# Two layers of scan, routed experts and retention on one core: own places in the first routed layer, and another order in the retention loop

## The chip, the cores and the metric

The kernel runs on one core of a Trainium2 chip. The metric is the device time of one execution in microseconds. Engines are named as in the profile: PE (TensorE), PEld (its weight loads), DVE (VectorE), ACT (ScalarE), POOL (GpSimd), SP (SyncE, which here only issues DMAs).

## The reference

An input of 8 sequences of 256 tokens with 128 features (2048 tokens) goes through two layers. Each layer normalizes its input to `xn` and adds two branches.

```
layer 0:  x = x + ssm(xn) + moe0(xn)
  ssm : up-projection, causal conv, silu, scan over 256 steps with 256 x 16 states, gate, down-projection
  moe0: scores = softmax(xn @ Wr)            # 8 experts
        G, idx = top_k(scores.T, 512)        # each EXPERT chooses 512 tokens
        h   = gelu(xn[idx] @ W1 + b1)        # 128 -> 512, per expert
        out[idx] += G * (h @ W2 + b2)        # 512 -> 128
layer 1:  x = x + retention(xn) + moe1(xn)
  retention: 8 heads of 16, q k v projections, scores = (q k^T) * decay mask, scores @ v,
             normalization per head, silu gate, output projection
  moe1: 16 experts, each token takes its best 2, relu, 128 -> 512 -> 128
```

## The kernel before

All five engines have programs written out by hand, each in the order of its code, and they meet at semaphores only. No scheduler decides anything. The stages follow each other: norms and the expert search of layer 0, the scan (one batch after another, 16 steps each, DVE the busiest), the first routed layer (moe0), layer 1's norm, retention, and the second routed layer.

**The first routed layer.** For expert e the steps are these. `one_hot(e)` on DVE (L505) compares the 16 x 8 places of the tokens with a row of numbers and writes a bf16 tile `hot[e]` of 128 x 2048. `compact(e)` on PE (L1010) multiplies it in 16 small matmuls into bank 7, which gives 512 token numbers. `indices(e)` on DVE (L513) adds and casts them into `idx`. `gather(e, q)` on POOL (L1633), four indirect DMAs of 128 rows each, brings the rows of `token_rows` (features and the 8 gates) into `xg`. `turn_rows(e)` on PE (L1088) transposes them into bank 6, and `rows_out(e)` on ACT copies them to `xgT`. `up0(e)` on PE (L1097) writes banks 0 to 3, `gelus(e)` on ACT makes `hbuf` of them, and `down0(e)` on PE (L1108) writes bank 4 or 5. `gated(e)` on DVE (L556) adds the bias row and multiplies by the gate into `ye` (two buffers). `put(e)` on POOL (L1686), four indirect DMAs, scatters `ye` into expert e's own table `expert_rows` in DRAM, which was zeroed earlier. `rows_in(e)` on SP (L831) loads that table of 1 MB back into one of two buffers, and `row_sum(e)` on DVE (L565) adds it to `acc`.

What sets the order is `expert_steps`, which runs a list of (lag, function) for s = 2 to 10 and calls each function with s - lag; every engine has its own list:

```
PE    turn_rows(0), then ((2, up0), (0, compact), (1, turn_rows), (3, down0))
DVE   ((0, one_hot), (0, indices), (3, gated), (5, row_sum))
ACT   rows_out(0), then ((2, gelus), (1, rows_out))
POOL  ((0, gathers), (3, put))
```

Experts 0 and 1 are compacted and gathered while the last batch of the scan still runs. Places are shared: `hot` has four (two in `xnT`, two in `gate`), so that `one_hot(e)` for e > 3 waits for `compact(e - 2)`; `xg` has four in `xm`, so that `gather(e)` for e > 3 waits for `gated(e - 4)`; weights and bias rows have two. SP loads the weights of expert e when expert e - 2 has let go of them (`weights1`, `weights2`, L792 and L797), in between the `rows_in`. The result of the scan is turned back by PE (L1086) in four groups through banks 0 and 1, and DVE adds it to `acc` (L552).

**Retention.** Per batch b: `project(b)` on PE (L1143) makes q and k in bank 4; ACT's `qk_out(b)` (L1481) copies them out; DVE's `query_decay(b)` (L682) takes its part; `scores(b)` on PE (L1155) writes banks 0 to 3; DVE's `decay(b, j)` (L690, four of them) multiplies by the mask into `pm`; `retain(b)` on PE (L1177) multiplies by v; ACT's `ret_out(b)` (L1500) copies it out. `scores(b)` waits until the four `decay(b - 1, j)` are done. In the loop PE runs scores(b), retain(b - 1), project(b + 1).

## Time and profile before

| | us |
|---|---|
| median of three runs | 796.07 (795.64 to 796.97) |
| the profiled execution | 797.28 |
| its span in the trace | 795.4 |
| scan's last down-projection leaves ACT | at 427.0 |
| first routed layer, to its last scatter | 427.0 to 538.6 |
| norm and projections of layer 1 | to 565 |
| routing of layer 1 on DVE | to 589 |
| retention | 589 to 660 |
| second routed layer and output | 660 to 795.4 |

The profiled execution lies 1.2 us above the median; 1.9 us of it lie outside the span. "Busy" is the time of instructions on an engine. For POOL it is the time in which it makes a DMA's descriptors, not the transfer. A row of the timeline gives start, duration, engine, line, operation and tiles, then the idle time before it and what ended that.

### The profile page before, as it was taken

How to read it: one execution, taken by the hardware profiler on the slowest of the kernel's cores; microseconds unless marked ns; L12 is line 12 of the kernel's file. 1: busy time of each engine (PE TensorE's matmuls, PEld its weight loads, DVE VectorE, ACT ScalarE, POOL GpSimd, SP SyncE). 2: the span in 40 equal slices, each digit the busy share in tenths (PEclk: the TensorE clock that was granted, in tenths of full speed). 3: DMA queues.
4: the chain of work that ended last, by engine and by line, in shares of the span. 5: the costliest groups of instructions: out<-in, count | busy, mean ns of one | idle time of the engine just before them, and what ended most of it. 6: DMA issues, size and time to landing. Idle time of an engine off the chain costs nothing.

```text
span 795.4 us, 12651 instructions
## 1 busy us (share of the span) xinstructions
PE 578.7 (73%) x3363; PEld 420.2 (53%) x3364; DVE 560.2 (70%) x1342; ACT 295.6 (37%) x706; POOL 392.6 (49%) x481
## 2 busy tenths in 40 slices
PE   4368874698888899879687776751637747999991
PEld 3222333466565666556464554641525426999991
DVE  7256589899999999999995225157475375665553
ACT  2532363664453546445312313120414432334430
POOL 1030036477676767767744578572137500444441
PEclk9999995899999999999796889785859975999996
DMA  9996000000000000000003346549501110212115
GB/s 187 210 315 189 1 3 0 2 0 2 1 1 0 0 0 0 0 0 0 1 5 115 91 132 198 158 135 316 205 15 51 45 27 5 57 48 55 50 30 158
DMA packets 59174, 55.83 MB, mean 70 GB/s; under 512 B 7871, under 2 KB 46166, under 8 KB 58880
## 3 DMA queue, kind: packets, MB, share of 16 engines
q1 hardware_dynamic: 53744, 43.61, 19.0%
q0 software_dynamic: 5392, 11.76, 5.8%
q8 instruction: 17, 0.28, 0.1%
q14 instruction: 21, 0.17, 0.1%
HBM read 35.27 MB, written 21.12 MB: 71 GB/s over the span
## 4 chain that ended last, share of the span: by engine, by line
PE 36%; DVE 31%; issue 6%; POOL 3%; DMA 3%; ACT 2%; DVEq 1%; SPq 1%; ACTq 0%; POOLq 0%
DVE arena L529 13%; PE bank L1287 7%; PE bank L1273 6%; DVE arena L490 6%; PE bank L1115 3%; PE bank L1038 3%; PE bank L1008 2%; PE bank L1040 2%; POOL expert_rows L1693 2%; DVE hbuf L725 2%; DMA xm<-token_rows,zbuf 2%; PE bank L978 1%; PE bank L1105 1%; POOL xm L1640 1%; PE bank L1166 1%
## 5 line engine op out<-in xcount | busy, mean ns | idle before, releaser
L529 DVE TENSOR_TENSOR_SCAN arena<-bank,arena 128x256 f32<-128x256 f32 x256 | 162.3, 679 | 5.2 <-issue 5.2
L1648 POOL TENSOR_TENSOR arena<-arena 128x256 f32<-128x256 f32 x128 | 99.4, 777 | 93.2 <-DVE arena L490 89.8
L1413 ACT ACTIVATE arena<-delta,nega 128x256 f32<-128x256 f32 (+1 forms) x256 | 107.7, 496 | 30.4 <-DVE arena L529 28.6
L490 DVE SCALAR_TENSOR_TENSOR arena<-arena,inva,bank 128x256 f32<-128x256 f32 x256 | 109.2, 471 | 0.0
L1038 PE MATMUL bank<-bd,xnw 128*128 128x258 f32 x256 | 88.6, 429 | 26.4 <-DVE arena L529 26.0
L1735 POOL DMA_INDIRECT pair_rows<-w1b,xnT x48 | 49.8, 1037 | 98.5 <-DVE w1b L761 95.2
L1008 PE MATMUL bank<-arena,ident 128*128 128x256 f32 x256 | 80.3, 398 | 20.3 <-DVEq L503 15.7
L1040 PE MATMUL bank<-bd,xnw 128*128 128x256 f32 x256 | 79.4, 393 | 0.0
L1629 POOL TENSOR_TENSOR bd<-cfs,btok 128x258 f32<-128x258 f32 x128 | 77.8, 628 | 0.0
L1038 PEld LDWEIGHTS bank<-bd,xnw 128*128 128x128 f32 x256 | 44.2, 198 | 56.0 <-DVE arena L529 40.4
L1008 PEld LDWEIGHTS bank<-arena,ident 128*128 128x128 f32 x256 | 44.6, 198 | 29.0 <-POOL arena L1648 25.2
L1287 PE MATMUL bank<-arena,hbuf 128*128 x384 | 56.5, 291 | 0.0
L1040 PEld LDWEIGHTS bank<-bd,xnw 128*128 128x128 f32 x256 | 50.9, 199 | 8.2
L1273 PE MATMUL bank<-xsT,xm 128*128 128x128 f32 x384 | 53.0, 283 | 0.9 <-DVE xm L744 0.9
L1693 POOL DMA_INDIRECT expert_rows<-gate,zbuf x32 | 41.0, 1281 | 22.9 <-DVE gate L563 14.3
L1273 PEld LDWEIGHTS bank<-xsT,xm 128*128 128x128 f32 x384 | 48.3, 198 | 1.9 <-DVE xm L744 1.8
L1287 PEld LDWEIGHTS bank<-arena,hbuf 128*128 128x128 f32 x384 | 47.3, 194 | 3.3
L1640 POOL DMA_INDIRECT xm<-token_rows,zbuf x32 | 39.0, 1219 | 18.3 <-DVE zbuf L517 9.7
L743 DVE COPY xm<-bd 128x512 f32 x48 | 20.6, 429 | 33.4 <-issue 31.0
L561 DVE TENSOR_TENSOR gate<-bank,zbuf 128x512 f32<-128x512 f32 x8 | 5.5, 692 | 51.6 <-PE bank L1115 51.4
L1115 PEld LDWEIGHTS bank<-w2b,hbuf 128*128 128x128 f32 x256 | 36.7, 232 | 0.5 <-issue 0.5
L1115 PE MATMUL bank<-w2b,hbuf 128*128 128x128 f32 x256 | 36.7, 314 | 0.0
(273 smaller groups left out, 1033.9 us busy)
## 6 DMA issues: line engine op xcount, KB each, us to landing
expert_rows<-bd SPq DMA_DIRECT2D x8, 1024.0 KB, 9.8
bd<-in_w SPq DMA_DIRECT2D x4, 1024.0 KB, 14.4
arena<-in_w SPq DMA_DIRECT2D x4, 1024.0 KB, 14.2
slots_in<-bd POOLq DMA_DIRECT2D x1, 3120.0 KB, 34.4
xnT<-slots_in SPq DMA_DIRECT2D x48, 65.0 KB, 1.8
w1b<-in_w SPq DMA_DIRECT2D x8, 256.0 KB, 6.4
w2b<-in_w SPq DMA_DIRECT2D x8, 256.0 KB
delta<-in_mask_d SPq DMA_DIRECT2D x1, 1664.0 KB
```

The costliest lines, as they stand in the source:

```text
L490: m = V.scalar_tensor_tensor(out=zb[:, s % 8, r, :], in0=zb[:, s % 8, r, :], scalar=inva[:, h, n:n + 1], in1=c_bank(n2)[:, r * L:(r + 1) * ...
L529: m = V.tensor_tensor_scan(zb[:, s % 8, r, :], dw_bank(par, s)[:, r * L:(r + 1) * L], abar[:, s % 8, r, :], 0.0, ALU.add, ALU.mult)
L1008: pe.matmul(Y[:, h * L:(h + 1) * L], ident[:, :], zb[:, s % 8, 0, :], start=(s == 0), stop=(s == 15), skip_group_check=True).then_inc(S["p ...
L1038: pe.matmul(o[:, :, 0:P + 1], xT[:, par, 0, h * P:(h + 1) * P], bd[:, par, 0, 2 * n2:2 * n2 + 2, :], start=True, stop=False, skip_group_ch ...
L1040: pe.matmul(o[:, :, P:L], xT[:, par, 1, h * P:(h + 1) * P], bd[:, par, 1, 2 * n2:2 * n2 + 2, 0:P], start=False, stop=True, skip_group_chec ...
L1115: m = pe.matmul(bank[4 + e % 2][:, q * P:(q + 1) * P], hbuf[:, e % 2, c, q * P:(q + 1) * P], w2b[:, e % 2, c, :], start=(c == 0), stop=(c ...
L1273: m = pe.matmul(bank[2 * (u % 2) + c // 2][:, c % 2 * P:(c % 2 + 1) * P], w1s[:, u % 2, c * P:(c + 1) * P], xsT[:, u % 2, :], start=True, ...
L1287: m = pe.matmul(bank[6 + u % 2][:, 0:P], hT[:, u % 2, c * P:(c + 1) * P], w2r[:, bass.ds(e, 1), c, :], start=False, stop=(c == HC - 1))
L1413: m = nc.scalar.activation(abar[:, s % 8, r, :], delta[:, h, bass.ds(b * L, L)], ACT.Exp, scale=negs[:, h, n:n + 1])
L1629: m = nc.gpsimd.tensor_tensor(bd[:, par, c, n, :], bid[:, None, :].broadcast_to([P, 2, P + 1]), btok[:, par, c, n, None].broadcast_to([P, ...
L1648: nc.gpsimd.tensor_tensor(zb[:, s % 8, 0, :], zb[:, s % 8, 0, :], zb[:, s % 8, 1, :], ALU.add).then_inc(S["q_ready"], 1)
L1693: nc.gpsimd.indirect_dma_start(out=moe[e], out_offset=bass.IndirectOffsetOnAxis(ap=idx[:, 4 * e + q:4 * e + q + 1], axis=0), in_=ye[:, e % ...
```

## The change

1. Routed layer: `hot[2]` to `hot[7]` get own places in `arena`, `xg[2]` to `xg[7]` own places in `bd`, and the weights of experts 2 to 5 own places in the other half of `bd`; SP loads those four when batch 6 of the scan has left `bd` (`dw_ready` at 7 x 16). Experts 6 and 7 take the places of 0 and 1. All eight bias rows come in one load, `b2r`. The waits that the shared places needed are gone.
2. DVE: `one_hot(2)` stands ahead of the four additions to `acc`; the other one-hots and indices follow at once, and only behind the last of them `gated` and `row_sum`.
3. PE: the turned result of the scan goes through four banks (2 to 5), so that its groups don't wait for DVE; the six compactions stand between the first steps of experts 0 and 1, and from expert 2 on the order is up0(e), turn_rows(e + 1), down0(e - 1).
4. POOL: gathers of experts 2, 3 and 4, then put(0), gathers of 5, put(1), gathers of 6, put(2), gathers of 7, put(3), and put(4) to put(7).
5. SP: `rows_in(0)` to `rows_in(7)` in a row, behind the loads of experts 6 and 7.
6. Retention: PE runs scores(b), project(b + 1), retain(b - 1); ACT runs qk_out(b), ret_out(b - 2), values_out(b).

The diff's core:

```diff
-        b2b = zf[:, 640:640 + 2 * P].rearrange("p (a d) -> p a d", a=2)
+        b2r = arena[:, 6144:6144 + E0 * P].rearrange("p (e d) -> p e d", e=E0)
...
-        xg = [xmf[:, o:o + 4 * ROW].rearrange("p (q r) -> p q r", q=4) for o in (0, 4 * ROW, T, 8 * ROW)]
+        bdf = bd[:, :, :, :, :].rearrange("p a c n t -> p (a c n t)")
+        xg = [f.rearrange("p (q r) -> p q r", q=4) for f in
+              [xmf[:, o:o + 4 * ROW] for o in (0, 4 * ROW)] + [bdf[:, 4128 + 4 * ROW * k:4128 + 4 * ROW * (k + 1)] for k in range(E0 - 2)]]
-        hots = [f.bitcast(BF16).rearrange("p (a t r) -> p a t r", a=2, t=NT) for f in (xnT[:, :], gate[:, 0, :])]
-        hot = [hots[e > 1][:, e % 2, :, :] for e in range(E0)]
+        hot = [f[:, o:o + NT * P // 2].bitcast(BF16).rearrange("p (t r) -> p t r", t=NT) for f, o in
+               [(xnT, 0), (xnT, NT * P // 2)] + [(arena, NT * P // 2 * k) for k in range(E0 - 2)]]
+        w1e = [w1b[:, e % 2, :] if e % 6 < 2 else bdf[:, 1024 * e - 2048:1024 * e - 1536] for e in range(E0)]
+        w2e = [w2b[:, e % 2, :, :] if e % 6 < 2 else
+               bdf[:, 1024 * e - 1536:1024 * e - 1024].rearrange("p (c d) -> p c d", c=HC) for e in range(E0)]
...
-                if e > 3:
-                    dve.wait_ge(S["cp_ready"], e - 1)
...
+            one_hot(2)
...
-                V.tensor_tensor(t, t, bank[q % 2][:, :], ALU.add).then_inc(S["dve_done"], 1)
+                V.tensor_tensor(t, t, bank[YM_BANK[q]][:, :], ALU.add).then_inc(S["dve_done"], 1)
...
+                if e == 0:
+                    dve.wait_ge(S["b2_in"], 16)
...
-                                     b2b[:, e % 2, None, :].broadcast_to([P, 4, P]), ALU.add))
-                V.tensor_tensor(y, y, xg[e % 4][:, :, P + e:P + e + 1].broadcast_to([P, 4, P]), ALU.mult).then_inc(S["ye_ready"], 1)
+                                     b2r[:, e, None, :].broadcast_to([P, 4, P]), ALU.add))
+                V.tensor_tensor(y, y, xg[e][:, :, P + e:P + e + 1].broadcast_to([P, 4, P]), ALU.mult).then_inc(S["ye_ready"], 1)
...
-            expert_steps(((0, one_hot), (0, indices), (3, gated), (5, row_sum)))
+            for e in range(AHEAD, E0):
+                indices(e)
+                if e + 1 < E0:
+                    one_hot(e + 1)
+            expert_steps(((3, gated), (5, row_sum)))
...
-            def weights1(e):
...
-            def weights2(e):
-                if e > 1:
-                    sp.wait_ge(S["ye_ready"], e - 1)
...
+            def weights(e):
+                mid = 1 < e < 6
+                if e > 5:
+                    sp.wait_ge(S["u_ready"], (e - 5) * HC)
+                sp.dma_start(w1e[e], w1_0[e, :, :]).then_inc(S["w_mid" if mid else f"w1_in{e % 2}"], 16)
+                if e > 5:
+                    sp.wait_ge(S["ye_ready"], e - 5)
+                sp.dma_start(w2e[e].rearrange("p c d -> p (c d)"), w2_0[e, :, :]).then_inc(S["w_mid" if mid else f"w2_in{e % 2}"], 16)
...
+            sp.wait_ge(S["dw_ready"], 7 * 16)
+            for e in range(2, 6):
+                weights(e)
...
             sp.wait_ge(S["dve_done"], 7)
+            sp.dma_start(b2r, b2_0.rearrange("e d -> (e d)").partition_broadcast(P).rearrange("p (e d) -> p e d", e=E0)
+                         ).then_inc(S["b2_in"], 16)
...
-
-            weights1(2)
-            for e in range(2, E0):
-                if e + 1 < E0:
-                    weights1(e + 1)
-                weights2(e)
-                rows_in(e - 2)
-            rows_in(E0 - 2)
-            rows_in(E0 - 1)
+                        sp.dma_start(staged[e % 2][:, 4 * q:4 * q + 4, :], src[:, 4 * q:4 * q + 4, :]).then_inc(S[f"pair_in{q}"], 16)
+
+            weights(6)
+            weights(7)
+            for e in range(E0):
+                rows_in(e)
...
-                pe.wait_ge(S["dve_done"], 3 if q < 2 else 2 + q)
+                if q == 0:
+                    pe.wait_ge(S["dve_done"], 3)
...
-                    else:
-                        pe.wait_ge(S["dve_done"], 7)
-                    pe.matmul(bank[c][:, :], w1b[:, e % 2, c * P:(c + 1) * P], xgT[:, e % 2, :], start=True, stop=True
+                    elif c > 1:
+                        pe.wait_ge(S["dve_done"], 4 + c)
...
-            expert_steps(((2, up0), (0, compact), (1, turn_rows), (3, down0)))
+            compact(2)
+            up0(0)
+            compact(3)
+            turn_rows(1)
+            compact(4)
+            up0(1)
+            compact(5)
+            pe.wait_ge(S["dve_done"], 7)
+            down0(0)
+            compact(6)
+            turn_rows(2)
+            compact(7)
+            for e in range(2, E0):
+                up0(e)
+                if e + 1 < E0:
+                    turn_rows(e + 1)
+                down0(e - 1)
+            down0(E0 - 1)
...
                     scores(b, par)
+                    project(i * 2 + (3 + par))
                     retain(i * 2 + (1 + par), 1 - par)
-                    project(i * 2 + (3 + par))
...
                     b = i * 2 + (2 + par)
+                    qk_out(b, par)
                     ret_out(i * 2 + par, par)
-                    qk_out(b, par)
...
-                    if e > 3:
-                        pool.wait_ge(S["ye_ready"], e - 3)
...
-            expert_steps(((0, gathers), (3, put)))
+            for e in range(AHEAD, E0):
+                for q in range(4):
+                    gather(e, q)
+                if e > 3:
+                    put(e - 4)
+            for e in range(E0 - 4, E0):
+                put(e)
```

Three places where the order of instructions moves.

POOL in the first routed layer, from the gathers of expert 3 on (`xm` and `bd` hold `xg`; `gate` holds `ye`). Before:

```order
L1640 DMA xm<-token_rows,zbuf 128x136 [waits id_ready,rows_g]
L1640 DMA xm<-token_rows,zbuf 128x136 x3
L1693 DMA expert_rows<-gate,zbuf 2048x128 [waits ye_ready]
L1693 DMA expert_rows<-gate,zbuf 2048x128 x3
L1640 DMA xm<-token_rows,zbuf 128x136 [waits ye_ready,id_ready,rows_g]
L1640 DMA xm<-token_rows,zbuf 128x136 x3
```

With the change:

```order
L1669 DMA bd<-token_rows,zbuf 128x136 [waits id_ready,rows_g]
L1669 DMA bd<-token_rows,zbuf 128x136 x3
L1718 DMA expert_rows<-gate,zbuf 2048x128 [waits ye_ready]
L1718 DMA expert_rows<-gate,zbuf 2048x128 x3
L1669 DMA bd<-token_rows,zbuf 128x136 [waits id_ready,rows_g]
L1669 DMA bd<-token_rows,zbuf 128x136 x3
```

The gathers of expert 4 stand ahead of the first scatter and wait for indices only; from expert 5 on gathers and scatters alternate as before, but one expert further on.

PE in the first routed layer, from `turn_rows(0)` on (L1094 and L1104 are `turn_rows`, L1019 and L1028 `compact`, L1105 and L1118 `up0`, L1115 and L1129 `down0`). Before:

```order
L1094 MATMUL bank<-ident,xm 128x128 [waits xg_in0]
L1094 MATMUL bank<-ident,xm 128x128 x3
L1105 MATMUL bank<-xm,w1b 128x512 [waits dve_done,xg_sb,w1_in0]
L1105 MATMUL bank<-xm,w1b 128x512 [waits dve_done] x3
L1019 MATMUL bank<-zbuf,gate 128x8 [waits id_ready,hot_ready]
L1019 MATMUL bank<-zbuf,gate 128x8 x15
L1094 MATMUL bank<-ident,xm 128x128 [waits xg_sb,xg_in1]
L1094 MATMUL bank<-ident,xm 128x128 x3
```

With the change:

```order
L1104 MATMUL bank<-ident,xm 128x128 [waits xg_in0]
L1104 MATMUL bank<-ident,xm 128x128 x3
L1028 MATMUL bank<-zbuf,arena 128x8 [waits id_ready,hot_ready]
L1028 MATMUL bank<-zbuf,arena 128x8 x15
L1118 MATMUL bank<-xm,w1b 128x512 [waits xg_sb,w1_in0]
L1118 MATMUL bank<-xm,w1b 128x512
L1118 MATMUL bank<-xm,w1b 128x512 [waits dve_done] x2
L1028 MATMUL bank<-zbuf,arena 128x8 [waits id_ready,hot_ready]
```

The first compaction now stands ahead of `up0(0)`, and down0(0) has four compactions ahead of it.

PE in the retention loop (L1166 and L1197 are `scores`, L1191, L1195, L1222 and L1226 `retain`, L1152 and L1183 `project`). Before:

```order
L1159 ISA [waits qk_sb]
L1166 MATMUL bank<-xm,w1b 128x128 [waits pm_ready]
L1166 MATMUL bank<-xm,w1b 128x128 x15
L1182 ISA
L1191 MATMUL bank<-zbuf,xm 32x128 [waits vs_sb,r_free,qd_sb,pm_ready]
L1191 MATMUL bank<-zbuf,xm 32x128 x15
L1195 MATMUL bank<-xm 32x128 x4
L1152 ISA [waits qd_sb]
L1152 MATMUL bank<-xnT,z2p 128x256 x2
```

With the change:

```order
L1190 ISA [waits qk_sb]
L1197 MATMUL bank<-xm,w1b 128x128 [waits pm_ready]
L1197 MATMUL bank<-xm,w1b 128x128 x15
L1183 ISA [waits qd_sb]
L1183 MATMUL bank<-xnT,z2p 128x256 x2
L1213 ISA
L1222 MATMUL bank<-zbuf,xm 32x128 [waits vs_sb,r_free,qd_sb,pm_ready]
L1222 MATMUL bank<-zbuf,xm 32x128 x15
L1226 MATMUL bank<-xm 32x128 x4
```

`project` has moved in between `scores` and `retain`.

## Rows read from the trace of the kernel before

**Rows 1.** The page: busy time of the engines over the span.

```profile
PE 578.7 (73%) x3363; PEld 420.2 (53%) x3364; DVE 560.2 (70%) x1342; ACT 295.6 (37%) x706; POOL 392.6 (49%) x481
```

**Rows 2.** Busy time by stretch: us, five engines, granted clock, DMA share, GB/s.

```profile
437.00:540.00 103.00, 67.77 (x416) 52.10 (x416) 37.40 (x38) 24.12 (x35) 71.75 (x56) 0.85 0.48 147
...
597.00:625.00 28.00, 19.43 (x412) 15.14 (x416) 14.34 (x27) 13.28 (x36) 20.20 (x24) 0.99 0.15 49
```

**Rows 3.** Waits, 431 to 540 us: engine, line, for whom; total, times, longest.

```profile
DVE gate L561 <- PE bank L1115: 51.4, 7, 12.0
...
POOL expert_rows L1693 <- DVE gate L563: 14.3, 4, 7.7
```

**Rows 4.** Groups of instructions, 431 to 540 us: busy, mean ns, idle before.

```profile
L1693 POOL DMA_INDIRECT expert_rows<-gate,zbuf x32 | 41.0, 1281 | 22.9 <-DVE gate L563 14.3 <-issue 8.5
...
L1640 POOL DMA_INDIRECT xm<-token_rows,zbuf x24 | 30.8, 1284 | 16.4 <-DVE zbuf L517 9.7 <-issue 6.1 <-DVE gate L563 0.6
...
L510 DVE TENSOR_TENSOR gate<-cfs,zbuf 128x2048 bf16<-128x2048 f32 x6 | 13.7, 2286 | 0.3 <-DVE acc L568 0.2
...
L568 DVE TENSOR_TENSOR acc<-acc,xnT 128x2048 f32<-128x2048 f32 x4 | 9.1, 2287 | 4.0 <-DMA xnT<-expert_rows 4.0
```

**Rows 5.** Timeline, from the end of the scan to the gathers of expert 2.

```profile
427.04 3.53 PE L1086 MATMUL bank<-ident,z2p 128*128 128x128 f32 x16 [0.65 <-ACT z2p L1403]
...
430.41 0.60 PE L1094 MATMUL bank<-ident,xm 128*128 128x128 f32 x4
...
435.25 0.55 PE L1019 MATMUL bank<-zbuf,gate 128*128 128x8 bf16 x16
...
436.95 2.27 POOL L1640 DMA_INDIRECT xm<-token_rows,zbuf  x1 [9.41 <-DVE zbuf L517]
```

**Rows 6.** Timeline, 440 to 470 us, PE, DVE and POOL.

```profile
445.05 1.12 PE L1094 MATMUL bank<-ident,xm 128*128 128x128 f32 x4 [3.97 <-DMA xm<-token_rows,zbuf]
...
445.95 5.94 PE L1115 MATMUL bank<-w2b,hbuf 128*128 128x128 f32 x32
...
456.50 3.74 PE L1115 MATMUL bank<-w2b,hbuf 128*128 128x128 f32 x32
...
460.07 3.60 PE L1105 MATMUL bank<-xm,w1b 128*128 128x512 f32 x8
...
461.61 2.28 DVE L510 TENSOR_TENSOR gate<-cfs,zbuf 128x2048 bf16<-128x2048 f32 x1
...
461.86 2.87 POOL L1640 DMA_INDIRECT xm<-token_rows,zbuf  x1 [0.30 <-DVE gate L563]
```

**Rows 7.** Timeline, the last scatter, and the sum behind it.

```profile
537.67 0.97 POOL L1693 DMA_INDIRECT expert_rows<-gate,zbuf  x1 [0.30 <-issue]
...
542.77 0.69 DVE L579 TENSOR_TENSOR acc<-acc,xnw 128x512 f32<-128x512 f32 x1 [1.19 <-DMA xnw<-expert_rows]
```

**Rows 8.** Timeline, one turn of the retention loop.

```profile
604.61 1.17 PE L1166 MATMUL bank<-xm,w1b 32*128 32x128 f32 x32 [1.45 <-ACT xm L1488]
...
605.72 1.08 PE L1191 MATMUL bank<-hbuf,xm 128*32 128x128 f32 x32
605.80 2.48 DVE L695 TENSOR_TENSOR zbuf<-bank,delta 128x512 f32<-128x512 f32 x4 [0.99 <-PE bank L1166]
606.48 0.96 POOL L1727 DMA_INDIRECT slots_in<-xnw,slot  x1 [0.30 <-issue]
...
606.95 1.13 PE L1152 MATMUL bank<-xnT,z2p 128*128 x4
...
608.57 0.83 ACT L1488 ACTIVATE xm<-bank,parity 128x256 f32<-128x256 f32 x2
...
609.53 1.17 PE L1166 MATMUL bank<-xm,w1b 32*128 32x128 f32 x32 [1.46 <-ACT xm L1488]
```

**Rows 9.** Timeline, `scores(1)`, ahead of the loop.

```profile
592.60 2.09 PE L1166 MATMUL bank<-xm,w1b 32*128 32x128 f32 x32 [1.54 <-DVE hbuf L695]
```

45 lines of the change are left out of this document (20 added, 25 removed).

## The prediction

> **What bounds the kernel now.** The page's busy shares come first [rows 1]: no engine is busy over three quarters of the span, so the stages must be read one by one. The view by stretch [rows 2] shows that in the first routed layer (437 to 540 us) POOL is the fullest engine, 71.75 us of 103, and PE has 67.77 at a granted clock of 0.85. POOL's work there is 24 gathers and 32 scatters [rows 4]. Next I read what it waits for [rows 3]: 14.3 us until DVE's `gated` has made rows to scatter, in 4 waits, the longest 7.7. DVE itself waits 51.4 us for `down0`. So neither engine is full: POOL stands still while an expert passes through PE, and PE stands still while POOL gathers the next one, since gather(e) stands behind put(e - 3) in POOL's order. After the stage everything hangs on the last scatter: it is issued at 537.67, and the last table's first quarter is in the sum at 542.77 [rows 7].
>
> The same rows give the price of a POOL DMA. One lasts 0.96 us and the next begins 0.30 later [rows 6, 8], so 1.27 us each. The mean is 1.28 us of busy time [rows 4], so something lengthens some of them. Rows 6 show what: DVE's L510 runs from 461.61 to 463.89, and the gather that begins at 461.86 takes 2.87 us, to 464.73, that is 0.84 us past the end of L510. L510 and L568 read two SBUF tiles for 2.29 us [rows 4]; when a POOL DMA begins within one, it starts its work at that one's end. DVE's L695 reads a PSUM bank, and the scatter at 606.48, inside its 2.48 us, takes its plain 0.96 [rows 8]. Of 71.8 us of POOL's busy time, 56 x 0.965 = 54.0 are its own and 17.8 are such holds, for 5 one-hots and 6 row sums that meet it, 1.6 us each.
>
> The Trainium skill bears on this (SBUF — State Buffer, section Who interferes with whom). It says that a DVE instruction with two SBUF inputs contends only with a GpSimd instruction that reads SBUF, and infers that a `tensor_tensor` leaves descriptor generation alone, since that needs the write port. By that inference the 17.8 us of holds would not exist, and the stream below would end at 506 instead of 524. The trace of before disagrees (2.87 us against 0.96), so the sum keeps them.
>
> **The routed layer, step by step.** From POOL's view the stage before is 436.95 to 538.64, 101.7 us: 71.1 for 56 DMAs at 1.27, 17.8 of holds, and 12.8 of waits.
>
> *Start.* Before, `compact(2)` begins on PE at 435.25 and POOL's first gather of expert 2 at 436.95, 1.70 later [rows 5]. Ahead of it stood `up0(0)`, and the one-hot behind DVE's four additions. Now `one_hot(2)` runs before the additions, and `compact(2)` stands right behind `turn_rows(0)`. The 16 transposes run from 427.04, and `turn_rows(0)` from 430.41 for 0.60 [rows 5]; four banks in place of two can only shorten that, I count nothing. 431.0 + 1.7 = 432.7: 4.25 us earlier. `one_hot(2)` now holds one of the gathers of expert 1, which lie before that and have slack.
>
> *Gathers first.* The gathers of 2, 3 and 4 need only indices. DVE makes those in a chain with PE: one-hot 2.29, compact 0.55, add and cast 0.4. Expert 3's indices come behind `up0(0)` (about 436.2), expert 4's some 3.4 us after (439.8), ahead of POOL in both cases. POOL takes 12 x 1.27 = 15.2 us plus four or five holds of 1.6, to about 455. Will put(0) be ready? `up0(1)` now waits for `compact(4)` to 439.1, `down0(0)` follows at about 443.2 and takes 3.74 or 5.94 us by the clock [rows 6]; `compact(6)`, `one_hot(7)` and `compact(7)` then stand ahead of `gated(0)` on DVE, which ends at 452.6 to 454.8. So its wait is about zero. This order makes `gated(0)` later than before (453.35), at no cost, since POOL has gathers to do.
>
> *The rest of the stream.* From then on POOL has 16 + 28 more DMAs. An expert costs PE 3.60 + 0.60 + 3.74 = 7.9 us at the high clock [rows 5, 6], POOL 10.2 us for a gather and a put and more with holds. So POOL is last. `gated(e)` needs put(e - 2) landed; that is one put and one gather away, and holds POOL up at most for moments. Of 12.8 us of waits I leave 2.5; the ends are 0 and 8. The holds stay at 17.8: as many one-hots (3 to 7) and row sums (0 to 5) meet the stream. If every one of the 11 hit fully it would be 25; if half missed, 9.
>
> Sum: 432.7 + 71.1 + 17.8 + 2.5 = 524.1 against 538.64, **14.5 us less**. Behind the last scatter nothing changes: `rows_in(7)`, quarters, norm. It would give back a little if the loads of 1 MB fell behind the faster puts; put after put takes 5.1 to 7 us, and the load of a table some 5.
>
> *Edits at nothing.* The 2 MB of weights for experts 2 to 5 load during batch 7 of the scan, where SP has nothing else; if they were late, `up0(2)` would wait, 90 us after their issue. The bias load goes ahead of the mask's 1.7 MB and delays it 2 us, needed 100 us later; `gated(0)`, the first to wait for the bias, comes 20 us after its issue. Experts 6 and 7 load in turns when 0 and 1 are through, 20 us and more before use. SP's `rows_in(0)` stands behind these two waits; `row_sum(0)` stands behind `gated(2)` anyway. Fewer semaphores and banks 2 to 5: `up0(0)` and `down0(0)` wait for the additions, which end before.
>
> **Retention.** One turn is 609.53 - 604.61 = 4.92 us [rows 8]: scores, from 605.72 `retain`, from 606.95 `project`, ACT's copies to 609.40, then the next scores. `retain` is in that chain for 1.23 us and feeds nothing in it. With `project` in front the chain is 1.11 + 2.58 = 3.69. Now the next in line: scores(b + 1) wait for the four `decay(b)`, which run from 605.80 to 608.28 [rows 8]; with 0.15 of signal that is 3.82 to 3.92 from scores to scores. PE's own work is 1.11 + 1.23 + 1.13 = 3.5 plus gaps of 0.2, also below. So a turn takes about 3.9, 1.0 less, in the 5 turns from scores(2) to scores(7): **5.0 us less**; the ends are 3 and 6. The 32 scatters of POOL there end at 632, well ahead of their use. What follows (gates, norm per head, projection) begins at the last `retain` and moves along whole.
>
> **The sum**: 14.5 + 5.0 = 19.5 us. Against the profiled execution 797.28 - 19.5 = 777.8; its own time is 1.2 us above the median, and against the median 796.07 the forecast is 776.6.
>
> **The rivals.**
> 1. *PE bounds the routed layer at its low clock.* Compactions and waits for rows leave gaps; before, the granted clock was 0.85 [rows 2], and after a wait of 3.97 us a `down0` took 5.94 and a turn 1.12 [rows 6]. From 439.1: 7 x 3.60 + 8 x 5.94 + 6 x 1.12 + 4 for compactions = 83.5, to 522.6, then `gated` and a last put of 8: 531. Gain 7.6 + 5.0: 783.5. Against it: such gaps mean that PE has time to spare. 0.16.
> 2. *The gathers meet the mask's load.* Twelve gathers in a row start with its transfer, before only after most of it. If POOL had to wait until it is through (about 441), 8 us are lost: 784.6. Before, gathers during it kept their pace. 0.05.
> 3. *Retention gains nothing*, since DVE or ACT in order takes `retain`'s place: 781.6. 0.07.
> 4. *More than I count*: no waits left, half of the holds missed: 524.1 - 2.5 - 5 = 516.6, and 6 from retention: 768. 0.05.
> 5. *Slower: PE at 1.2 GHz in the retention loop.* scores(1) took 2.09 us ahead of the loop [rows 9] against 1.17 within, where the granted clock was 0.99 [rows 2]. If the new order let it fall, PE's 3.5 us of a turn become 6.2 and with gaps 6.6, 1.7 x 6 = 10 us more; with rival 1's gain of 7.6 that is 798.5. It decides when the loop's granted clock is below about 0.6. Against it: PE is busier than before in every turn. 0.02. The Trainium skill (TensorE: Matmul & The Clock Gate, Part 1) has it that activity releases the throttle, so by it the loop would keep the high clock.
> 6. *It changes nothing*, because rows come back in step with the loads of 1 MB: 0.01.
>
> **How the numbers follow.** The forecast has 0.64. Its own bounds (waits 0 to 8, holds 9 to 25, retention 3 to 6) rarely add up and give 771 to 784. With rivals 1 to 3 on the high side and 4 on the low one, the range for 8 in 10 is 770.5 to 785. 0.2% (1.6 us) is about what a measurement of this kernel tells from no change: faster 0.97, same 0.01, slower 0.02.
>
> **What would show it.** The first gather of expert 2 at about 432.7 of the span; 12 gathers in a row; no POOL wait for `gated` over 3 us; POOL's long DMAs still ending 0.84 us after a two-input DVE instruction; the last scatter's end at 524; scores to scores 3.9 us, with DVE's `decay` ending right before. Wrong it is if `down0` mostly takes 5.9 us and POOL waits for it (rival 1), if gathers of expert 2 are long with DVE idle (2), or if a turn stays at 4.9 (3).

## The result, and the profile after

| | before | changed |
|---|---|---|
| median of four runs, us | 796.08 (795.64 to 796.97) | 775.16 (773.63 to 776.99) |
| the profiled execution | 797.28 | 776.99 |
| its span | 795.4 | 775.2 |

The ratio of the runs is 0.9755, with a 95% interval of 0.9729 to 0.9782: 19.5 us less (17.4 to 21.6). The two medians by themselves are 20.9 apart, which this interval takes in. The forecast was 776.6, the range 770.5 to 785.

The profile after, in the order of the rows before. First the page's busy line and the view by stretch over the routed stage, cut where the first scatter starts (us; PE, PEld, DVE, ACT, POOL busy; granted clock, DMA share, GB/s):

```profile
PE 579.2 (75%) x3363; PEld 419.8 (54%) x3364; DVE 559.7 (72%) x1342; ACT 295.0 (38%) x706; POOL 393.5 (51%) x481
```
```profile
427.00:456.00 29.00, 23.63 (x182) 15.72 (x181) 17.52 (x24) 10.73 (x16) 21.42 (x14) 0.87 0.47 149
456.00:523.00 67.00, 46.95 (x286) 36.11 (x284) 23.49 (x20) 18.75 (x28) 52.78 (x45) 0.90 0.51 153
```

The busy times are those of [rows 1] within 1 us: no work was taken away. From 456 to 523 us POOL is busy 52.78 of 67 us, and its 45 DMAs leave a gap of 0.30 us each: it hardly stands still. PE is busy 46.95 of the 67. The waits and the groups from 427 to 522 us say so too (for each wait: engine and tile waiting, for whom; total, times, longest):

```profile
DVE gate L568 <- PE bank L1129: 21.5, 4, 7.5
...
POOL expert_rows L1718 <- issue: 9.5, 31, 0.3
```
```profile
L1718 POOL DMA_INDIRECT expert_rows<-gate,zbuf x32 | 40.7, 1270 | 10.5 <-issue 9.5 <-DVE gate L570 1.1
L1669 POOL DMA_INDIRECT bd<-token_rows,zbuf x24 | 31.2, 1299 | 10.9 <-issue 6.4 <-DVE zbuf L521 4.5
```

The scatters' wait for `gated` was 14.3 us in 4 waits [rows 3]; it is 1.1 in one. DVE's own wait for `down0` fell from 51.4 us to 21.5. What has not changed is the length of the DMAs: 1270 and 1299 ns are those of before [rows 4]. 40.7 + 31.2 - 56 x 0.965 = 17.9 us of holds (17.8 before).

The timeline at the start and the end of the stage:

```profile
427.69 0.47 ACT L1434 ACTIVATE z2p<-bank,colv 128x256 f32<-128x256 f32 x1 [21.90 <-PE bank L1086]
...
431.44 0.60 PE L1104 MATMUL bank<-ident,xm 128*128 128x128 f32 x4
...
431.88 0.55 PE L1028 MATMUL bank<-zbuf,arena 128*128 128x8 bf16 x16
...
433.58 2.26 POOL L1669 DMA_INDIRECT bd<-token_rows,zbuf  x1 [3.92 <-DVE zbuf L521]
```
```profile
448.38 2.29 DVE L514 TENSOR_TENSOR arena<-cfs,zbuf 128x2048 bf16<-128x2048 f32 x1
...
451.60 0.69 DVE L568 TENSOR_TENSOR gate<-bank,arena 128x512 f32<-128x512 f32 x1
```
```profile
449.00 2.50 POOL L1669 DMA_INDIRECT bd<-token_rows,zbuf  x1 [0.30 <-issue]
...
456.85 1.00 POOL L1718 DMA_INDIRECT expert_rows<-gate,zbuf  x1 [0.30 <-issue]
...
509.82 0.97 POOL L1718 DMA_INDIRECT expert_rows<-gate,zbuf  x1 [1.07 <-DVE gate L570]
...
521.99 0.97 POOL L1718 DMA_INDIRECT expert_rows<-gate,zbuf  x1 [0.31 <-issue]
```

`compact(2)` stands right behind `turn_rows(0)`, and the first gather of expert 2 begins 433.58 - 431.88 = 1.70 us after it, as before. The gather at 449.00 begins within the one-hot of 448.38 to 450.67 and ends at 451.50, 0.83 after it: the hold of [rows 6]. `gated(0)` starts at 451.60, 5.25 us before POOL comes to its scatter at 456.85; the only wait in the whole stream is the 1.07 before 509.82.

The retention loop, PE and then DVE:

```profile
599.27 1.17 PE L1197 MATMUL bank<-xm,w1b 32*128 32x128 f32 x32 [0.36 <-DVE zbuf L706]
600.37 1.13 PE L1183 MATMUL bank<-xnT,z2p 128*128 128x256 f32 x4
601.43 1.08 PE L1222 MATMUL bank<-zbuf,xm 128*32 128x128 f32 x32
602.33 0.40 PE L1226 MATMUL bank<-xm 128*32 128x128 f32 x8
603.06 1.17 PE L1197 MATMUL bank<-xm,w1b 32*128 32x128 f32 x32 [0.33 <-DVE hbuf L706]
```
```profile
600.43 2.49 DVE L706 TENSOR_TENSOR hbuf<-bank,delta 128x512 f32<-128x512 f32 x4 [1.09 <-PE bank L1197]
602.87 0.29 DVE L699 TENSOR_TENSOR xm<-bank,delta 128x128 f32<-128x128 f32 x1
```

A turn is 603.06 - 599.27 = 3.79 us against 4.92 [rows 8]. The scores waited for ACT's L1488 before; now they wait for DVE: `decay` ends at 602.92, 0.14 before them.

Where the time went, with `scan` for the start of ACT's last down-projection copy (427.69 above). The first five rows are spans from one event to the next and the sixth what follows; together they are the difference of the spans, 795.4 - 775.2.

| stretch | before | after | |
|---|---|---|---|
| start to scan | 426.51 | 427.69 | +1.2 |
| scan to first gather of expert 2 | 10.44 | 5.89 | -4.5 |
| that gather to the last scatter's end | 101.7 | 89.4 | -12.3 |
| last scatter's end to the first projection of retention | 50.4 | 50.7 | +0.3 |
| that projection to the gates, behind the loop | 40.7 | 35.0 | -5.7 |
| gates to the end | 165.7 | 166.6 | +0.9 |

In the fourth stretch 0.9 us are given back at once: from the last scatter's end to L590's first addition 5.04 us pass, against 4.13 for L579 [rows 7].

### The profile page after: what moved, and what is told of

Same layout as the page of the kernel before. It is cut to its first block, busy times and chain, and to the rows that moved or that the text cites. A ratio compares the mean times of both kernels' runs of the same rounds, so it can differ in the third digit from the quotient of the medians.

```text
span 775.2 us, 12645 instructions
## 1 busy us (share of the span) xinstructions
PE 579.2 (75%) x3363; PEld 419.8 (54%) x3364; DVE 559.7 (72%) x1342; ACT 295.0 (38%) x706; POOL 393.5 (51%) x481
## 4 chain that ended last, share of the span: by engine, by line
PE 33%; DVE 29%; POOL 8%; issue 7%; DMA 3%; ACT 2%; DVEq 1%; SPq 1%; POOLq 0%; ACTq 0%
DVE arena L533 12%; PE bank L1318 7%; PE bank L1304 6%; DVE arena L496 5%; POOL expert_rows L1718 4%; PE bank L1047 4%; PE bank L1017 3%; POOL bd L1669 3%; PE bank L1049 3%; DVE hbuf L736 2%; PE bank L987 1%; DMA xnw<-expert_rows 1%; PE bank L1197 1%; DVE hbuf L706 1%; PE bank L1316 1%
## 5 line engine op out<-in xcount | busy, mean ns | idle before, releaser
L1017 PE MATMUL bank<-arena,ident 128*128 128x256 f32 x256 | 81.9, 405 | 20.3 <-DVEq L509 15.7
L1049 PE MATMUL bank<-bd,xnw 128*128 128x256 f32 x256 | 81.5, 402 | 0.0
L1047 PEld LDWEIGHTS bank<-bd,xnw 128*128 128x128 f32 x256 | 45.8, 202 | 51.1 <-DVE arena L533 35.3
L1017 PEld LDWEIGHTS bank<-arena,ident 128*128 128x128 f32 x256 | 45.4, 201 | 29.2 <-POOL arena L1677 25.2
L1049 PEld LDWEIGHTS bank<-bd,xnw 128*128 128x128 f32 x256 | 52.4, 205 | 8.7
L1718 POOL DMA_INDIRECT expert_rows<-gate,zbuf x32 | 40.7, 1270 | 10.5 <-issue 9.5
L1669 POOL DMA_INDIRECT bd<-token_rows,zbuf x24 | 31.2, 1299 | 10.9 <-issue 6.4
L907 PE MATMUL bank<-ident,xnw 128*128 128x128 f32 x32 | 7.9, 394 | 38.2 <-DVEq L327 38.2
L1758 POOL DMA_INDIRECT slots_in<-xnw,slot x32 | 30.7, 961 | 9.9 <-issue 9.2
L955 PE MATMUL bank<-z2p,delta 128*128 x64 | 34.9, 672 | 0.0
```

The source lines that it names most:

```text
L1017: pe.matmul(Y[:, h * L:(h + 1) * L], ident[:, :], zb[:, s % 8, 0, :], start=(s == 0), stop=(s == 15), skip_group_check=True).then_inc(S["p ...
L1047: pe.matmul(o[:, :, 0:P + 1], xT[:, par, 0, h * P:(h + 1) * P], bd[:, par, 0, 2 * n2:2 * n2 + 2, :], start=True, stop=False, skip_group_ch ...
L1049: pe.matmul(o[:, :, P:L], xT[:, par, 1, h * P:(h + 1) * P], bd[:, par, 1, 2 * n2:2 * n2 + 2, 0:P], start=False, stop=True, skip_group_chec ...
L1669: nc.gpsimd.indirect_dma_start(out=xg[e][:, q, :], out_offset=None, in_=rows, in_offset=bass.IndirectOffsetOnAxis(ap=idx[:, 4 * e + q:4 * ...
L1718: nc.gpsimd.indirect_dma_start(out=moe[e], out_offset=bass.IndirectOffsetOnAxis(ap=idx[:, 4 * e + q:4 * e + q + 1], axis=0), in_=ye[:, e % ...
```

## The experiments

Twelve kernels ran, in three groups. `ret_alone` is an edit of the kernel before, `control` the changed kernel itself, the others edits of the changed kernel; each stood beside runs of the kernel before on its chip. That kernel's median was 793.71 us beside `ret_undone`, `ret_pe_only`, `pool_undone` and `compact_undone`, 796.75 beside `ret_alone`, `weights_late`, `no_row_sum` and `quarters` (another chip), and 793.18 beside the last four. So medians compare within such a group only, and across groups the ratios do. The stage numbers of their profiled executions, taken as above ("last" is the end of the last scatter after the scan's end; "holds" is POOL's busy time for the 56 DMAs less 56 x 0.965; "turn" is the mean from scores to scores in the loop):

| kernel | scan | first gather | last | holds | turn | median | ratio to before (95%) |
|---|---|---|---|---|---|---|---|
| before | 426.5 | 10.4 | 112.1 | 17.8 | 4.9 | 796.08 | |
| changed | 427.7 | 5.9 | 95.3 | 17.9 | 3.8 | 775.16 | 0.9755 (0.9729 to 0.9782) |
| ret_undone | 424.9 | 6.6 | 96.0 | 18.5 | 4.9 | 778.51 | 0.9796 (0.9758 to 0.9834) |
| ret_pe_only | 423.8 | 6.0 | 96.9 | 19.4 | 5.2 | 780.39 | 0.9824 (0.9790 to 0.9859) |
| ret_alone | 427.4 | 10.4 | 111.8 | 18.0 | 3.8 | 791.00 | 0.9934 (0.9908 to 0.9960) |
| pool_undone | 422.8 | 5.9 | 101.9 | 18.4 | 3.8 | 779.42 | 0.9830 (0.9786 to 0.9873) |
| compact_undone | 423.8 | 10.3 | 106.5 | 12.7 | 3.8 | 783.66 | 0.9870 (0.9833 to 0.9907) |
| weights_late | 423.9 | 5.9 | 96.4 | 18.9 | 3.8 | 775.07 | 0.9755 (0.9704 to 0.9806) |
| no_row_sum | 428.5 | 5.9 | 86.6 | 8.4 | 3.8 | 767.46 | 0.9649 (0.9599 to 0.9700) |
| control | 424.5 | 5.9 | 96.1 | 18.7 | 3.8 | 775.52 | 0.9770 (0.9749 to 0.9792) |
| quarters | 426.0 | 6.6 | 90.6 | 4.5 | 3.8 | 772.34 | 0.9711 (0.9649 to 0.9773) |
| rows_quarters | 423.4 | 6.6 | 90.2 | 9.9 | 3.8 | 770.62 | 0.9722 (0.9706 to 0.9738) |
| hots_quarters | 426.0 | 6.6 | 93.8 | 10.6 | 3.8 | 772.05 | 0.9731 (0.9707 to 0.9756) |
| gated_early | 423.8 | 6.6 | 87.1 | 4.0 | 3.8 | 767.24 | 0.9669 (0.9656 to 0.9682) |

The first thing to see is the scan's column. None of these edits touches the scan's instructions, and its end lies anywhere from 422.8 to 428.5; the changed kernel itself has 427.7 in one execution and 424.5 in another (`control`). So a difference of 3 us between two medians may be the scan's, and the columns behind it, which count from its end, tell more. The same holds for ratios: the changed kernel has 0.9755 in its own runs and 0.9770 as `control`. What an edit costs is given below against 0.9755; against `control` each such figure is 0.15%, or 1.2 us, smaller.

The first gather is at 5.9 in some of these kernels and at 6.6 in others, also where the edit lies elsewhere (`ret_undone`). It goes with PE's clock: in the 29 us from the scan's end the mean granted clock was 0.87 in the changed kernel and in `control`, and 0.79 in `ret_undone` and `quarters`. There `turn_rows(0)` took 1.06 us in place of 0.60.

### Retention: both orders back, one order back, and the orders alone

`ret_undone`, the loop's part on each engine (the peeled end alike):

```diff
                     scores(b, par)
-                    project(i * 2 + (3 + par))
                     retain(i * 2 + (1 + par), 1 - par)
+                    project(i * 2 + (3 + par))
...
-                    qk_out(b, par)
                     ret_out(i * 2 + par, par)
+                    qk_out(b, par)
```

> The changed kernel with both orders of the retention loop put back (PE: scores, retain, project; ACT: ret_out, qk_out, values_out), the routed layer left as changed. Theory: the turn from scores to scores goes from 3.80 us back to about 4.9, and the time rises by 5.4 us over the changed kernel, to about 780.6; the routed layer's last scatter stays where it is. Rival (the retention loop was only a bystander, and its shorter turns come from something ahead of it): the turn stays at 3.8 and the time at 775.

`ret_pe_only` has the second hunk alone:

> The changed kernel with ACT's order in the retention loop put back (ret_out ahead of qk_out), and PE's new order kept. Theory: qk_out of batch b then waits behind ret_out of the batch before, which PE's new order makes late, so the next scores wait for both; the turn goes to 5.3 us or so, slower than with both orders old (4.9), and the time to about 782.7. Rival (the order on ACT is irrelevant, PE's order makes the gain): the turn stays at 3.8 and the time at 775.

`ret_alone` is the kernel before with both hunks the other way round:

> The kernel before with the retention loop's two new orders alone; the routed layer is as it was. Theory: the turn falls from 4.88 us to 3.8 and the time by 5.4 us, to about 790.7, so that this part of the change and the routed part add up to the whole. Rival (the two parts meet, the gain needs the other part): 796 or 793.

Measured: turns of 4.88 us in `ret_undone` (4.83 to 4.92), 5.18 in `ret_pe_only` (5.13 to 5.22), 3.80 in `ret_alone`. PE and ACT in `ret_pe_only`:

```profile
597.22 0.38 ACT L1534 ACTIVATE hbuf<-bank 128x256 f32 x1 [3.11 <-PE bank L1226]
597.50 0.38 ACT L1517 ACTIVATE w1b<-bank 128x256 f32<-128x256 f32 x1
597.76 0.84 ACT L1519 ACTIVATE xm<-bank,parity 128x256 f32<-128x256 f32 x2
```
```profile
594.63 1.13 PE L1183 MATMUL bank<-xnT,z2p 128*128 x4
...
596.59 0.40 PE L1226 MATMUL bank<-xm 128*32 128x128 f32 x8
598.74 1.17 PE L1197 MATMUL bank<-xm,w1b 32*128 32x128 f32 x32 [1.75 <-ACT xm L1519]
```

`ret_out` (L1534) waits 3.11 us for the end of `retain`, and `qk_out` (L1517, L1519), whose input had been there since PE's L1183 ended at 595.76, stands behind it. So PE's order gains nothing without ACT's, and costs 0.3 us a turn more than the old pair. Five turns make that 6.9 us over the changed kernel; by the ratios `ret_pe_only` lies 0.69% of the kernel before above it, 5.5 us, and `ret_alone` 0.66% below the kernel before, 5.3 us. `ret_undone` lies only 0.41% above (3.3 us), where its turns say 5.4; its interval is 0.4% to either side. The loop's gain needs nothing of the routed part, and the other way round. ACT's new order with PE's old one wasn't tried.

### The POOL order back

```diff
-                if e > 3:
-                    put(e - 4)
-            for e in range(E0 - 4, E0):
+                if e > 2:
+                    put(e - 3)
+            for e in range(E0 - 3, E0):
```

> The changed kernel with the scatters of an expert put back to one expert's gathers earlier on the POOL queue (gathers of e, then scatters of e-3), everything else kept. Theory: the waits of the queue for gated come back, since the gated rows of expert e-3 are not written by then: 4 to 9 us of waits in all in front of L1718, the last scatter about 7.8 us later, the time about 783. Rival (the own places and the waits that they took away suffice, the order of the queue is worth nothing): waits in front of the scatters stay near 1 us, and the time at 775.

POOL's waits for `gated`, from the view of waits, and two of them in the timeline:

```profile
POOL expert_rows L1718 <- DVE gate L570: 8.0, 4, 5.5
```
```profile
448.45 1.00 POOL L1718 DMA_INDIRECT expert_rows<-gate,zbuf  x1 [1.80 <-DVE gate L570]
...
504.63 2.77 POOL L1718 DMA_INDIRECT expert_rows<-gate,zbuf  x1 [5.46 <-DVE gate L570]
```

8.0 us of waits against 1.1, the last scatter 5.8 to 6.6 us later (101.9 against 96.1 and 95.3), the ratio up by 0.0075, 6.0 us (4.8 against `control`). The rival falls: places of their own let the gathers run ahead, but the queue must also be told to use it. Of my 7.8 us some four fifths came. What is left without this order is still 112.1 - 101.9 = 10.2 us of the 16.9.

### The compactions back in the steps

```diff
-            compact(2)
-            up0(0)
-            compact(3)
...
-                down0(e - 1)
-            down0(E0 - 1)
+            expert_steps(((2, up0), (0, compact), (1, turn_rows), (3, down0)))
```

and on DVE `one_hot` and `indices` of experts 3 to 7 back in the steps beside `gated` and `row_sum`.

> The changed kernel with compact(e) of experts 2 to 7 put back into the expert steps on PE, and the one-hots and indices of experts 3 to 7 on DVE beside them as before, so that a gather of expert e waits for the step of e again; the own places and the POOL order stay. Theory: the gathers of experts 3 and later are held back by the chain of row_sum, one_hot, compact, indices, which runs through each step; the last scatter comes about 11 us later and the time is about 786. Rival (the places alone, not the early compacts, freed the queue): the wait in front of the gathers stays that for the zero fill, and the time stays near 775.

```profile
434.05 2.27 POOL L1652 DMA_INDIRECT bd<-token_rows,zbuf  x1 [8.32 <-DVE zbuf L521]
...
454.17 0.95 POOL L1652 DMA_INDIRECT bd<-token_rows,zbuf  x1 [9.03 <-DVE zbuf L521]
```
```profile
POOL bd L1652 <- DVE zbuf L521: 21.1, 4, 9.0
```

L521 is the cast of `indices`. The first gather again starts 10.3 us after the scan, 4.4 later than in the changed kernel, and the first gather of expert 4 waits 9.03 us for its indices, 454.17. Against that 5 us of holds are gone; some one-hots now run while POOL stands still anyway. Together the last scatter is 10.4 to 11.2 us later, the ratio 0.9870 (9.2 us, or 8.0 against `control`). So the rival falls too, and the early compactions are the largest single part of the change that an edit took back. What is left without them is 112.1 - 106.5 = 5.7 us. With the 10.2 of `pool_undone` that makes 15.9 of 16.9: the two orders nearly add up, and each earns its part without the other. What the own places earn with both orders old wasn't tried.

### The weights late

The wait and the four `weights(e)` of SP moved behind the bias load, that is from 374.6 us of the changed kernel's profile to 429.0 here.

> The changed kernel with the weights of experts 2 to 5 sent out behind the bias load at the start of the routed layer (about 433 us) instead of during the last batches of the scan; they still go to places of their own. Theory: up0(2) starts some 30 us later than that, so the weights are in place all the same and the time stays at 775 (within 1); the early issue earned nothing by itself, and it did not slow the scan either. Rival one (the weights at 433 us meet the first gathers, the mask load and the zero fill, and the gathers' rows come late): slower by 1 to 3 us. Rival two (the early weights slowed the scan, whose end came 1.16 us later in the changed kernel than in the one before): faster by 1 us, the scan's end back at 427.0.

```profile
432.50 0.65 SPq L810 DMA_DIRECT2D bd<-in_w  x1
```
```profile
447.40 5.38 PE L1117 MATMUL bank<-xm,bd 128*128 128x512 f32 x8
```

The last of the eight is issued at 432.50, and `up0(2)`, the first that needs one, runs at 447.40 with no wait: 15 to 18 us behind the issue, not 30 as I wrote. Ratio and stage are those of the changed kernel. The early issue earned nothing, and with 423.9 beside the 424.5 of `control` it does not slow the scan. The 1.2 us at the table's head was scatter between executions.

### The holds: row sums left out

```diff
-                link(V.tensor_tensor(acc[:, :, :], acc[:, :, :], staged[e % 2], ALU.add))
                 dve.sem_inc(S["row_sum"], 1)
```

> The changed kernel with the row sums of experts 0 to 6 left out (the addition of the transposed rows into the accumulator; those experts are then missing from the output). Theory: the six holds that fall on row sums go from the POOL queue's stream and those of the one-hots stay: the holds fall from 17.9 us to about 8, the last scatter comes about 9 us earlier; at most some of it is lost to waits for gated, and the time is about 769 or less. Rival (the long POOL DMAs have nothing to do with DVE's operations): the long DMAs stay where they were and the time stays at 775.

The rows of experts 0 to 6 are missing from the output here. The groups of POOL, 430 to 520 us:

```profile
L1717 POOL DMA_INDIRECT expert_rows<-gate,zbuf x32 | 31.3, 977 | 11.3 <-issue 9.1 <-DVE gate L570 2.1
L1668 POOL DMA_INDIRECT bd<-token_rows,zbuf x24 | 31.2, 1299 | 10.9 <-issue 6.4 <-DVE zbuf L521 4.5
```

The scatters fall from 1270 to 977 ns on average, the gathers, which meet the one-hots, keep their 1299. So the scatters' holds were DVE's additions, all but 0.4 us: 31.3 + 31.2 - 54.0 = 8.5 us are left of 17.9, and the last scatter comes 8.7 to 9.5 us earlier. This shows what they cost the kernel, not yet how to be rid of them.

### The holds: the same operations in four pieces

`quarters`, on `one_hot` and in the same way on `row_sum` (there with the wait for `dve_link` behind the four):

```diff
-                V.tensor_tensor(hot[e], iota_p[:, None, :].broadcast_to([P, NT, P]),
-                                place[:, :, e:e + 1].broadcast_to([P, NT, P]), ALU.is_equal).then_inc(S["hot_ready"], 1)
+                for k in range(4):
+                    t = slice(4 * k, 4 * k + 4)
+                    m = V.tensor_tensor(hot[e][:, t, :], iota_p[:, None, :].broadcast_to([P, 4, P]),
+                                        place[:, t, e:e + 1].broadcast_to([P, 4, P]), ALU.is_equal)
+                m.then_inc(S["hot_ready"], 1)
```

> The changed kernel with each one-hot comparison and each row sum written as four instructions on a quarter of the columns each. Theory (an indirect DMA of POOL that begins while DVE runs a two-input operation on SBUF ends only 0.84 us after that operation does, so the length of the operation sets the hold): a hold falls from 1.0 to 1.9 us to some 0.6 us at most, the eleven holds of 17.9 us in all to about 11 to 12, and the time by 5 to 6.4 us to about 769.5. Rival one (each DVE instruction holds the one DMA that it meets by the same amount, so four short ones hold four DMAs): no gain, 775, or slower, to 780. Rival two (the hold comes from the data's traffic, not from the operation): four short ones hold the same DMA all through, and nothing changes.

A row sum of it, and the gather that begins within it:

```profile
471.94 2.50 DVE L580 TENSOR_TENSOR acc<-acc,xnT 128x512 f32<-128x512 f32 x4 [0.99 <-DMA xnT<-expert_rows]
```
```profile
472.74 1.32 POOL L1675 DMA_INDIRECT bd<-token_rows,zbuf  x1 [0.30 <-issue]
```
```profile
L1724 POOL DMA_INDIRECT expert_rows<-gate,zbuf x32 | 33.2, 1037 | 17.3 <-issue 8.8 <-DVE gate L573 8.4
L1675 POOL DMA_INDIRECT bd<-token_rows,zbuf x24 | 25.3, 1056 | 13.7 <-DVE zbuf L524 7.3 <-issue 6.4
```

Four pieces of 0.69 us in 2.50 start 0.60 apart, so the second ends at about 473.23. The gather ends at 474.06, 0.83 after that piece and while the next ones run. So the hold is by the instruction, and a DMA gets through between two of them. Both rivals fall: the same hold for each instruction would have given more holds in all, and one hold through all four pieces would have ended behind the last one. The holds are 4.5 us in all; I had put them at 11 to 12, too high even by my own bound, since eleven of at most 0.6 us are 6.6. But the last scatter came only 4.7 to 5.5 us earlier, not 13.4: waits for `gated` have grown from 1.1 to 8.4 us. Waits for indices have grown too, from 4.5 to 7.3 (L524 above). The largest wait is the one ahead of the very first scatter:

```profile
454.82 1.00 POOL L1724 DMA_INDIRECT expert_rows<-gate,zbuf  x1 [5.15 <-DVE gate L573]
```

The gathers ahead of it are through 5 us sooner, and `gated(0)` is not. Most of what the one-hots' holds cost was slack. By the time alone `quarters` isn't told from the changed kernel: its ratio, 0.9711, has an interval of 0.9649 to 0.9773, which holds the 0.9755.

### Each kind of pieces alone, and gated(0) earlier

`rows_quarters` and `hots_quarters` have one half each of that edit.

> The changed kernel with the row sums alone in four pieces, the one-hots whole. Theory: the five holds on one-hots stay (8.1 us over the plain length), those on row sums shrink from 9.7 us to about 2 to 3; the first scatter starts where it did (29.2 us after the scan's end), because the slow gathers fill the time in which gated(0) is awaited anyway; waits of 2 to 3 us for gated return at the end; the last scatter comes 4 to 6 us earlier and the time is 770 to 771, no worse than with both in pieces. Rival (the pieces of the one-hots earned it): 774 to 775.

> The changed kernel with the one-hots alone in four pieces, the row sums whole. Theory: the holds on one-hots shrink from 8.1 us to about 1.5, but the scatters of expert 0 wait for gated(0), which DVE makes behind the last indices, so nearly all of it turns into a wait of 5 us in front of L1718; the last scatter comes 0 to 1.5 us earlier, the time is 774 to 775. Rival (the holds on one-hots delay the stream as those on row sums do): 6 us earlier, 769.

`gated_early` has both, and besides

```diff
+                if e + 1 == E0:
+                    gated(0)
+                    one_hot(e)
                 indices(e)
-                if e + 1 < E0:
+                if e + 2 < E0:
                     one_hot(e + 1)
-            expert_steps(((3, gated), (5, row_sum)))
+            expert_steps(((3, next_gated), (5, row_sum)))
...
-            compact(7)
             for e in range(2, E0):
                 up0(e)
+                if e == 2:
+                    compact(7)
```

(`next_gated` leaves out expert 0.)

> Both in pieces as in the run with quarters, and gated(0) on DVE ahead of the one-hot and the indices of expert 7, with compact(7) on PE behind up0(2). Theory: gated(0) is ready 3 us earlier, so of the 5.15 us wait in front of the first scatter some 2 us are left, and the stream of 83.9 us shortens by up to 3; part of it comes back as waits for gated(6) and gated(7), since PE's steps set those. The time is 1 to 3 us below that with quarters, about 769 to 771 where quarters are 772. Rival (the end of the stream is set by PE alone): the same as with quarters.

> The changed kernel itself, run beside the others on the same chip as their yardstick. Theory: 0.9755 of the kernel before, within 0.003, about 775 to 777; holds of 17.6 us over the plain length of a POOL DMA and 0.8 us of waits for gated. The pieces' worth is then read from kernels that ran side by side. Rival (chips differ by more than the pieces are worth): its ratio to the kernel before lies below that of the run with quarters.

The scatters' group in `rows_quarters`, `hots_quarters` and `gated_early`, in this order:

```profile
L1721 POOL DMA_INDIRECT expert_rows<-gate,zbuf x32 | 33.1, 1034 | 12.5 <-issue 9.1 <-DVE gate L570 3.3
```
```profile
L1721 POOL DMA_INDIRECT expert_rows<-gate,zbuf x32 | 39.6, 1237 | 14.6 <-issue 9.4 <-DVE gate L573 5.1
```
```profile
L1733 POOL DMA_INDIRECT expert_rows<-gate,zbuf x32 | 32.7, 1022 | 14.4 <-issue 8.8 <-DVE gate L573 5.6
```

Row sums in pieces: holds 8.8 us less than in `control`, waits 2.2 more, the last scatter 5.9 earlier (90.2 against 96.1; 5.1 against the first profile), as with both. One-hots in pieces: 8.1 us less of holds, but 4.0 more of waits for `gated` (5.1, all ahead of the first scatter, against 1.1); the last scatter is 1.5 to 2.3 us earlier. By the medians they look nearly alike (770.6 and 772.1), their intervals overlap, and the 772.1 is lower than the 774 to 775 that I gave it; the stage numbers are what tells them apart. The interval of `rows_quarters` (0.9706 to 0.9738) lies clear of that of `control` (0.9749 to 0.9792), that of `hots_quarters` (0.9707 to 0.9756) doesn't.

In `gated_early` the second half of `gated(0)` starts at 448.14, before `one_hot(7)`, and the wait ahead of the first scatter is 1.73 us:

```profile
448.14 0.69 DVE L573 TENSOR_TENSOR gate<-gate,xm 128x512 f32<-128x512 f32 x1
448.75 2.49 DVE L516 TENSOR_TENSOR arena<-cfs,zbuf 128x512 bf16<-128x512 f32 x4
```
```profile
449.11 1.20 POOL L1733 DMA_INDIRECT expert_rows<-gate,zbuf  x1 [1.73 <-DVE gate L573]
```

The last scatter is 3.4 us ahead of `quarters`, 8.9 ahead of `control`. With 767.24 us it beats both kernels: 0.9669 of the kernel before (0.9656 to 0.9682) where `control` on the same chip has 0.9770 (0.9749 to 0.9792), so the two intervals lie 0.67% apart. 767.24 / 775.52 is 1.1% less, 8.3 us. Against `quarters` its ratio is 0.42% lower, 3.4 us, where I had expected 1 to 3 (the intervals of the two overlap); the 767.24 lies below my 769 to 771. `gated(0)` earlier without the pieces wasn't tried.

What is left there is at the end. The wait ahead of the scatters of expert 6 is 2.87 us, and DVE's rows show for whom:

```profile
495.09 2.56 DVE L580 TENSOR_TENSOR acc<-acc,xnw 128x512 f32<-128x512 f32 x4 [5.66 <-DMA xnw<-expert_rows]
497.87 0.69 DVE L571 TENSOR_TENSOR gate<-bank,arena 128x512 f32<-128x512 f32 x1 [0.21 <-DVE acc L580]
```

`gated(6)` stands behind a row sum on DVE, and that waited 5.66 us for its table. `gated(6)` ahead of it might earn up to 2.6 us. That wasn't tried, and stays open.

## Why the prediction was right

**The sum.** Forecast -14.5 for the routed layer and -5.0 for retention. Measured from the scan's end on: 112.1 - 95.3 = 16.9, and 5.4 in five turns. Less 0.9 us behind the last scatter, that is 21.4 us; the 20.2 between the spans are this, the 1.2 by which the scan ended later, and small differences elsewhere. The medians have 20.9 between them; the ratio has 19.5 with an interval that holds the 19.5 of the forecast, and `control`'s ratio has 18.3. The mechanism held, but that 19.5 meets 19.5 to the tenth is luck: the stages together gave 2 us more than forecast.

- *Start*: 4.25 forecast, 4.55 measured from the scan's end, with the chain as it was worked out (the transposes into four banks took 3.39 us in place of 3.53).
- *Gathers first*: put(0) begins 29.2 us after the scan, where the forecast's 455 meant 28.5. `gated(0)` ended at 453.0, in the 452.6 to 454.8 given (counted from the scan's end 0.8 us ahead of it), and POOL came 3.8 us later. `down0(0)` took 3.82 us. `pool_undone` and `compact_undone` show that each order earns its part.
- *Waits*: this term was mis-sized. I left 2.5 us, and 0.8 are there above the plain gap, in one wait; this makes 1.7 us of the 2.4 by which the routed layer beat its forecast. The start makes 0.3, and the rest is the DMAs' own pace, which I had rounded up (71.1 for 56; 56 x 0.965 + 55 x 0.30 = 70.5). And it was for another cause than I named: `gated(6)` waited for the row sum ahead of it on DVE, as in `gated_early` above, and that row sum for its table. In the changed kernel:

```profile
505.62 2.29 DVE L575 TENSOR_TENSOR acc<-acc,xnw 128x2048 f32<-128x2048 f32 x1 [5.46 <-DMA xnw<-expert_rows]
508.13 0.69 DVE L568 TENSOR_TENSOR gate<-bank,arena 128x512 f32<-128x512 f32 x1 [0.21 <-DVE acc L575]
```

The cause that I named came too, but at no cost to POOL: `gated(5)` waited 3.5 us for a landed put and was ready before its scatters' turn.
- *Holds*: 17.8 forecast, 17.9 measured. The rule behind them (a POOL DMA that begins within a DVE instruction on two SBUF tiles ends 0.84 us after it) held in the changed kernel for all eleven, at 0.81 to 0.85 us. It held for one more, which I had not listed: the scatter at 515.22 lasts 1.33 us, to 516.55, 0.85 after the end of the second half of `gated(7)` (515.01 to 515.70), which reads two SBUF tiles as well. The kernel before has two such, of 1.41 us at 502.00 and of 1.33 at 528.57, so its 17.8 us belong to 13 DMAs and not to the 11 that I counted. One gather doesn't fit: it begins at 488.98, 0.01 us into the second half of a `gated`, and takes its plain 0.95, while that DVE instruction takes 0.73 in place of 0.69. The experiments brought the holds down in two ways, to 8.5 by leaving row sums out and to 4.5 by pieces. The Trainium skill (SBUF — State Buffer, section Who interferes with whom) infers that a `tensor_tensor` leaves descriptor generation alone. For these indirect DMAs the runs contradict that: with the additions gone the scatters' mean falls from 1270 to 977 ns, where by that inference both should be equal. The same section's rule, that a DVE instruction with two SBUF inputs contends with a GpSimd instruction that reads SBUF, would cover them if the reading of their row numbers counts (`zbuf` stands among their inputs); the only POOL DMA of this kernel without row numbers runs at 2.73 us, where DVE has no such instruction, so that stays open.
- *Edits at nothing*: the weights' early issue is worth nothing either way (`weights_late`). `up0(2)` followed it by 77 us (374.6 to 451.1), not 90.
- *The tail*: I wrote that it would give back a little if the loads fell behind the puts. It gave back 0.9 us in this execution: the landing of the last scatter took 3.09 us in the chain of waits, 2.23 before. But the 5.04 us behind the last scatter were 4.12 in `ret_undone`, 4.72 in `control`, 4.92 in `ret_pe_only` and 5.38 in `weights_late`, which all have the same code there, against 4.13 in the kernel before and 4.10 in `ret_alone`. So up to all of it can be chance, and what sets the landing stays open.
- *Retention*: 3.9 forecast with DVE's `decay` as the next bound, 3.80 measured with just that in the rows. That a turn would fall only if ACT's order went along was not in the text; `ret_pe_only` shows it, at 5.2 us.

**The rivals.** PE at its low clock (rival 1) had PE last; the granted clock was 0.87 and 0.90 in the stage, `down0` took 3.74 to 3.82 us but for one of 4.95 (and one `up0` 5.38), and POOL never waited for it: its one wait was for the row sum. The mask load (2) did not lengthen a gather: those that meet no one-hot took 0.95 us. Retention (3) gained. More than I count (4) came true in its waits alone. Its sum had a slip: half of the holds are 8.9 us and not 5, which would have made it about 764. PE's clock in the loop (5) stayed high, with the granted clock (behind the busy times) at 1.00:

```profile
584.00:608.00 24.00, 20.95 (x492) 16.57 (x492) 16.25 (x30) 12.38 (x34) 17.23 (x20) 1.00 0.15 49
```
